# Bias of an attention kernel summed by VectorE from PSUM, maxima turned by VectorE, small products in reduced fp32

## The reference

```python
x = x + attention(_gn(x), W_qkv, W_out, b_out)
# attention, for one image, n = 4096 positions, c = 256 channels:
q, k, v = split(x @ W_qkv)                       # each n x c
k = softmax(k over the positions)
context = k.T @ v                                # c x c
out = (q @ context as in einsum('bde,bdn->ben')) @ W_out + b_out
```

## Time and profile before

| | |
|---|---|
| median of three runs | 1215.44 us |
| the profiled execution | 1214.93 us |
| its span, first to last instruction | 1213.2 us |
| PE busy | 1190.1 us, 98% of the span |
| DVE busy | 842.1 us, 69% |
| ACT busy | 840.1 us, 69% |
| POOL busy | 622.4 us, 51% |
| DMA | 63.5% of 16 engines' span, 220 GB/s |

### The profile page before, as it was taken

The page is one execution under the profiler, slowest core; times in us unless marked ns, Lnnn a source line. Parts: engine busy times, 40 slices in busy tenths (PEclk is TensorE's granted clock), DMA queues, the critical chain, the costliest instruction groups (busy, mean ns, idle before and its releaser), DMA issues.

```text
span 1213.2 us, 21447 instructions
## 1 busy us (share of the span) xinstructions
PE 1190.1 (98%) x8460; PEld 1115.8 (92%) x8460; DVE 842.1 (69%) x1582; ACT 840.1 (69%) x1140; POOL 622.4 (51%) x288
## 2 busy tenths in 40 slices
PE   4999999999999999999999999999999999999998
PEld 4998999999899998999989999899999989999897
DVE  6877667676776767768776677766767676676551
ACT  5767768677685776757677686776857768577664
POOL 8664564635645355563655636356463564536520
PEclk9999999999999999999999999999999999999999
DMA  9448666576765758666486665867657576573524
GB/s 339 146 167 294 218 235 205 195 269 208 274 203 199 264 172 294 226 206 237 162 301 229 221 227 183 286 209 252 204 201 263 193 278 225 201 252 122 191 74 170
DMA packets 107077, 266.71 MB, mean 220 GB/s; under 512 B 10208, under 2 KB 10208, under 8 KB 106976
## 3 DMA queue, kind: packets, MB, share of 16 engines
q1 hardware_dynamic: 106976, 265.33, 63.5%
HBM read 198.18 MB, written 67.11 MB: 219 GB/s over the span
## 4 chain that ended last, share of the span: by engine, by line
PE 93%; DVE 2%; ACT 1%; POOL 1%; DMA 1%; issue 1%; SPq 0%; DVEq 0%; POOLq 0%; ACTq 0%
PE ps_k L399 29%; PE ps_e L564 19%; PE ps_e L573 10%; PE ps_g L492 5%; PE ps_e L480 5%; PE ps_e L492 5%; PE ps_e L482 5%; PE ps_g L480 4%; PE ps_g L482 4%; PE ps_g L511 1%; PE ps_g L528 1%; PE ps_g L542 1%; PE ps_g L534 1%; POOL x_lo L347 1%; DVE mx L892 1%
## 5 line engine op out<-in xcount | busy, mean ns | idle before, releaser
L341 POOL TENSOR_TENSOR xt_lo<-xt_raw,xt_hi 128x1024 fp32r<-128x1024 f32 x128 | 307.4, 2404 | 434.5 <-ACT xt_hi L676 309.1
L347 POOL TENSOR_TENSOR x_lo<-x_raw,x_hi 128x1024 fp32r<-128x1024 f32 x128 | 281.4, 2216 | 65.6 <-ACT x_hi L681 56.2
L892 DVE TENSOR_TENSOR mx<-ps_k,mx 128x256 f32<-128x256 f32 x480 | 203.3, 424 | 95.8 <-ACT e_raw L685 74.3
L733 ACT ACTIVATE o_stage<-ps_e,bias 128x512 f32<-128x512 f32 x253 | 170.9, 689 | 114.1 <-PE ps_e L573 114.1
L399 PE MATMUL ps_k<-wk_hi,xt_hi 128*128 128x256 f32 x1024 | 207.1, 284 | 1.0 <-DVE mx L892 0.7
L399 PE MATMUL ps_k<-wk_lo,xt_hi 128*128 128x256 f32 x1024 | 205.5, 283 | 0.0
L685 ACT ACTIVATE e_raw<-ps_k 128x512 f32<-128x512 f32 x256 | 141.4, 596 | 87.2 <-PE ps_k L399 87.2
L849 DVE BATCH_NORM_STATS2 bn<-xs 128x6 f32<-128x512 f32 x240 | 154.5, 686 | 40.7 <-DMA xs<-in_xt_dram 39.5
L693 ACT ACTIVATE e_hi<-e_raw 128x1024 fp32r<-128x1024 f32 x128 | 135.1, 1055 | 60.9 <-DVE e_raw L917 33.0
L399 PEld LDWEIGHTS ps_k<-wk_hi,xt_hi 128*128 128x128 f32 x1024 | 163.4, 190 | 8.7 <-issue 1.8
L399 PE MATMUL ps_k<-wk_hi,xt_lo 128*128 128x256 f32 x1024 | 158.2, 283 | 0.0
(11 more groups left out here) (129 smaller groups left out, 1992.7 us busy)
## 6 DMA issues: line engine op xcount, KB each, us to landing
xt_raw<-in_xt_dram SPq DMA_DIRECT2D x128, 512.0 KB, 4.3
x_raw<-in_xn_dram SPq DMA_DIRECT2D x128, 512.0 KB, 3.5
out_dram<-o_stage SPq DMA_DIRECT2D x127, 512.0 KB, 4.5
xs<-in_xt_dram SPq DMA_DIRECT2D x240, 256.0 KB, 5.1
w_setup<-in_w_dram SPq DMA_DIRECT2D x2, 256.0 KB, 10.1
out_dram<-o_stage SPq DMA_DIRECT2D x2, 256.0 KB, 2.0
wk<-in_w_dram SPq DMA_DIRECT2D x1, 256.0 KB, 9.9
wq_t<-in_w_dram SPq DMA_DIRECT2D x1, 256.0 KB, 10.9
```

What stands on the lines that cost most here:

```text
L341: nc.gpsimd.tensor_tensor(xt_lo[:, s], xt_raw[:, s], xt_hi[:, s].bitcast(F32), ALU.subtract).then_inc(xt_lo_ready, 1)
L347: nc.gpsimd.tensor_tensor(x_lo[:, s], x_raw[:, s], x_hi[:, s, :, 0:C].bitcast(F32), ALU.subtract).then_inc(x_lo_ready, 1)
L733: nc.scalar.activation(o_stage[:, u % O_SLOTS, h, :], src, ACT.Identity, bias=bias[:, h:h + 1]).then_inc(o_ready, 1)
L892: nc.vector.tensor_tensor(mx[:], tile, mx[:], ALU.max).then_inc(max_done, 1)
```

## The change

- **Maxima.** DVE transposes `mx` itself, in squares of 32 x 32 (`nc.vector.transpose`), reduces each row of 32, brings the four quarters of the partitions together with three moves and reduces again. `m_blk` is now 32 partitions x 8. A move is a `tensor_reduce` over an axis of one element.
- **Spread.** DVE splits `m_blk` into two parts, one for fp32r and the rest, on 64 partitions, and multiplies them with two stacked identities (`block_diag`); PE spreads them with one fp32r product of 256 columns and ones.
- **Scales.** `dm` and `alpha` are made in the new layout, and four moves (`spread_scales`, before `take_first`) bring `alpha` back to channels on partitions.
- **Statistics.** For images from 1 on, mean and variance are split into two parts by DVE and averaged by one fp32r product each; `mean_of` and `var_of` add the two results.
- **Bias.** `bias_sum` is gone from PE. DVE scales the two rows of the matrix in PSUM with `neg_mean * rstd`, adds them, transposes, reduces, moves, adds b_out, and moves again.
- **Order.** On PE both `emit_high` of output 0 stand ahead of its `emit_low`. POOL waits for `diag_ready` of block 1 ahead of xt_low(n, 0), and of the next block 0 ahead of xt_low(n, 5). ACT makes four small copies at the start. In PE's stream `turn_max` is gone; the maxima wait for `turned_ready` on DVE's own side.
- `turned` and `b_terms` lie in the memory of `u_hi`, `diag` in its second half.

```diff
@@ gpsimd, period
+                pool.wait_ge(diag_ready, b * 2 + 2)
                 if more:
                     xt_low(n, np_, 0)
...
                     for j in range(3, NCH):
+                        if j == HALF + 1:
+                            pool.wait_ge(diag_ready, n * 2 + 1)
                         xt_low(n, np_, j)
@@ tensor
-            def turn_max(b, blk):
...
             def spread_max(b, blk):
...
+                pe.wait_ge(diag_ready, b * 2 + (blk + 1))
+                nc.tensor.matmul(max_psum(b, blk)[:, 1, 0:C], one_r[0:2 * Q].broadcast_to([2 * Q, P]), diag,
+                                 start=True, stop=True).then_inc(bc_ps, 1)
             def stats_mean(b):
...
+                    pe.wait_ge(max_done, b * (TILES * NCH))
+                    pe.wait_ge(mean_parts_ready, b)
+                    nc.tensor.matmul(stats_psum(b, 0), grp_r[:], mean_parts[:].rearrange("p k c -> p (k c)"), start=True,
+                                     stop=True).then_inc(mean_ps, 1)
             def stats_var(b):
...
+                    pe.wait_ge(var_parts_ready, b)
+                    nc.tensor.matmul(stats_psum(b, 1), grp_r[:], var_parts[:].rearrange("p k c -> p (k c)"), start=True,
+                                     stop=True).then_inc(var_ps, 1)
-            def bias_sum(b, parity):
...
                 emit_high(b, parity, 0, 0)
-                bias_sum(b, parity)
+                emit_high(b, parity, 0, 1)
                 emit_low(b, parity, 0, 0)
-                emit_high(b, parity, 0, 1)
                 emit_low(b, parity, 0, 1)
@@ vector
+            def move(to, values):
+
+                return nc.vector.tensor_reduce(to, values.unsqueeze(len(values.shape)), AX_X, ALU.max)
...
+                if b > 0:
+                    dve.wait_ge(mv_ready, b + 1)
+                    move(mean_parts[:, 0, :], mv[:, :, 0]).then_inc(mean_hi_ready, 1)
+                    dve.wait_ge(mean_hi_ready, b)
+                    nc.vector.tensor_tensor(mean_parts[:, 1, :], mv[:, :, 0], mean_parts[:, 0, :].bitcast(F32),
+                                            ALU.subtract).then_inc(mean_parts_ready, 1)
             def mean_of(b, parity):
...
+                    nc.vector.tensor_scalar(mean_rest[:], sums[:, CB:2 * CB], -1.0, None,
+                                            ALU.mult).then_inc(mean_rest_ready, 1)
+                    dve.wait_ge(mean_rest_ready, b)
+                    nc.vector.scalar_tensor_tensor(out=neg_mean[:, parity, :], in0=sums[:, 0:CB], scalar=-1.0,
+                                                   in1=mean_rest[:], op0=ALU.mult, op1=ALU.add).then_inc(mean_sum_ready, 1)
+                    dve.wait_ge(mean_sum_ready, b)
+                    nc.vector.tensor_tensor(dev[:], mv[:, :, 0], neg_mean[:, parity, :], ALU.add).then_inc(mean_read, 1)
...
+                if b > 0:
+                    dve.wait_ge(var2_ready, b + 1)
+                    move(var_parts[:, 0, :], var2[:]).then_inc(var_hi_ready, 1)
+                    dve.wait_ge(var_hi_ready, b)
+                    nc.vector.tensor_tensor(var_parts[:, 1, :], var2[:], var_parts[:, 0, :].bitcast(F32),
+                                            ALU.subtract).then_inc(var_parts_ready, 1)
             def block_max(b, blk):
...
+                n = b * 2 + blk + 1
+                dve.wait_ge(max_done, n * (TILES * HALF))
+                nc.vector.transpose(turned[:], mx[:]).then_inc(turned_ready, 1)
+                dve.wait_ge(turned_ready, n)
+                nc.vector.tensor_reduce(quad[:, :, 0], turned[:].rearrange("p (q k) -> p q k", k=Q), AX_X,
+                                        ALU.max).then_inc(quad_ready, 1)
+                dve.wait_ge(quad_ready, n)
+                for r in range(1, QUADS):
+                    last = move(quad[0:Q, :, r], quad[r * Q:(r + 1) * Q, :, 0])
+                last.then_inc(quad_moved, 1)
+                dve.wait_ge(quad_moved, n)
+                nc.vector.tensor_reduce(m_blk[:, blk, :], quad[0:Q], AX_X, ALU.max).then_inc(m_blk_ready, 1)
+
+            def block_diag(b, blk):
+                n = b * 2 + blk + 1
+                dve.wait_ge(m_blk_ready, n)
+                move(m_parts[0:Q, :], m_blk[:, blk, :]).then_inc(m_part_hi_ready, 1)
+                dve.wait_ge(m_part_hi_ready, n)
+                nc.vector.tensor_tensor(m_parts[Q:2 * Q, :], m_blk[:, blk, :], m_parts[0:Q, :].bitcast(F32),
+                                        ALU.subtract).then_inc(m_part_lo_ready, 1)
...
+                dve.wait_ge(m_part_lo_ready, n)
+                nc.vector.tensor_tensor(diag.rearrange("p (q k) -> p q k", k=Q),
+                                        eye2[:].unsqueeze(1).broadcast_to([2 * Q, NQ, Q]),
+                                        m_parts[:].bitcast(F32).unsqueeze(2).broadcast_to([2 * Q, NQ, Q]),
+                                        ALU.mult).then_inc(diag_ready, 1)
             def bias_of(b):
...
+                dve.wait_ge(scaled_mean_ready, b + 1)
+                nc.vector.tensor_scalar(b_terms[:, 0, :], ps_g0[:, 0, 0:C], scaled_mean[:, 0:1], None,
+                                        ALU.mult).then_inc(b_first_ready, 1)
+                dve.wait_ge(b_first_ready, b + 1)
+                nc.vector.scalar_tensor_tensor(out=b_terms[:, 0, :], in0=ps_g0[:, 1, 0:C], scalar=scaled_mean[:, 1:2],
+                                               in1=b_terms[:, 0, :], op0=ALU.mult, op1=ALU.add).then_inc(b_terms_ready, 1)
+                dve.wait_ge(b_terms_ready, b + 1)
+                nc.vector.transpose(b_terms[:, 1, :], b_terms[:, 0, :]).then_inc(b_turned_ready, 1)
...
             def gather_steps(b, parity, more):
                 n, np_ = b + 1, 1 - parity
                 block_max(b, 1)
+                block_diag(b, 1)
                 if more:
                     mean_of(n, np_)
                 block_scales(b)
-                mean_bias(b, parity)
                 shift(b, 4)
                 if more:
                     var_of(n)
                 e_low(b, 3)
                 shift(b, 5)
                 e_low(b, 4)
+                spread_scales(b)
                 take_first(b)
```

More of the change, by code:

```diff
@@ L107, in build @@
         u_lo = sb("u_lo", [P, CB, C], F32R)
+        with nc.sbuf_tensor("turned", [P, C], F32) as turned:
+            pass
+        with nc.sbuf_tensor("b_terms", [P, CB, C], F32) as b_terms:
+            pass
         u_hi = sb("u_hi", [P, CB, C], F32R)
+        diag = u_hi[0:2 * Q, 1, :]
         m_lo = u_lo
@@ L536, in combine_m @@
                     last.then_inc(m_ps, 1)
-            def bias_sum(b, parity):
-                pe.wait_ge(m_full_ready, b + 1)
-                for h in range(CB):
-                    for c in range(CB):
-                        last = nc.tensor.matmul(ps_g0[:, 0, h:h + 1], m_full[:, c, h * P:(h + 1) * P],
-                                                neg_mean[:, parity, c:c + 1], start=(h == 0 and c == 0),
-                                                stop=(c == CB - 1), skip_group_check=True)
-                last.then_inc(bias_ps, 1)
             def out_psum(b, u, h):
@@ L702, in scales @@
                 act.wait_ge(dm_ready, b + 1)
-                nc.scalar.activation(alpha[:], dm[:], ACT.Exp).then_inc(alpha_ready, 1)
+                nc.scalar.activation(alpha_q[:], dm[:], ACT.Exp).then_inc(alpha_q_ready, 1)
             def wk_high(b, parity):
@@ L739, in emit @@
                         emit_half(b, u, h)
+            act.wait_ge(consts_ready, 5)
+            nc.scalar.activation(grp_r[:], grp[:], ACT.Copy).then_inc(grp_r_ready, 1)
+            nc.scalar.activation(one_r[:], one_col[:], ACT.Copy).then_inc(one_r_ready, 1)
+            for r in range(2):
+                last = nc.scalar.activation(eye2[r * Q:(r + 1) * Q, :], ident[r * Q:(r + 1) * Q, r * Q:(r + 1) * Q],
+                                            ACT.Copy)
+            last.then_inc(eye2_ready, 1)
             for j in range(NCH):
@@ L908, in block_scales, with spread_scales @@
                 dve.wait_ge(m_all_ready, b + 1)
-                nc.vector.tensor_tensor(dm[:], m_blk[:], m_all[:].unsqueeze(1).broadcast_to([P, 2, CB]),
+                nc.vector.tensor_tensor(dm[:], m_blk[:], m_all[:].unsqueeze(1).broadcast_to([Q, 2, NQ]),
                                         ALU.subtract).then_inc(dm_ready, 1)
+            def spread_scales(b):
+                dve.wait_ge(alpha_q_ready, b + 1)
+                by_quad = alpha_q[:].rearrange("p k (d r) -> p k d r", r=QUADS)
+                for r in range(QUADS):
+                    last = move(alpha[r * Q:(r + 1) * Q, :, :], by_quad[:, :, :, r])
+                last.then_inc(alpha_ready, 1)
             def shift(b, j):
@@ L1105, in period @@
                 block_max(n, 0)
+                block_diag(n, 0)
                 bn_halves(8, 12)
```

157 lines of the change are left out of this document (105 added, 52 removed).

## The result

The changed kernel takes **1241.27 us** (median of 4 runs, 1237.64 to 1241.58), beside 1215.59 for the kernel before on the same chip: ratio 1.0209, 95% interval 1.0183 to 1.0234. One of the four executions of the kernel before took 4129.46 us and is left out of the ratio; the others lie between 1214.12 and 1215.74. The forecast was 1224, slower, with a range from 1199 to 1238: the sign was right, the size 17 us short, and the time lies outside the range. The profiled execution took 1241.58, its span is 1239.9.

A forecast was written before the change was run, and what follows sets the result against it. PE was taken to bound the kernel (93% of the chain). Per image +1.0 - 0.5 gave +7.7 over 14 images, image 15 +0.9, image 0 nothing: +8.6 on the median 1215.44, thus 1224 us, range 1199 to 1238.

The forecast's parts named there:

- Place one: Variance product: POOL's xt_low holds DVE's dev, so PE goes on 1.0 us later per image (bounds +0.7 to +1.5).
- Place two: Emission: bias chain of 3.4 us on DVE delays statistics and loads; PE still keeps 0.5 us an image.
- the landing of the loads: Third batch of xs loads, before the later outputs: lands 0.3 us later (bounds -0.6 to +1.3).
- the queue is full from there on: Emission: DMA is full behind the first output's store and the xt load, so the landing was taken as +0.3.
- My row for a full queue: Profile row cited for the loads: DMA at 0.99 of its time from 615 to 620 us.
- rival (c): Emission: bias chain delays the loads by its store, 1.3 us; +1.5 us per image, 1237 us, chance 0.18.
- PE's savings: Work PE no longer does: 2.1 us an image, 29 us over 14 images if nothing else ended later.
- the term for the spread: Spread of a maximum on PE: one pass of 0.12 to 0.15 us instead of 0.44, saving 0.3, twice an image.
- The mean product and the turn: PE in the gather: the turn's 0.2 us goes, and the mean product falls from 0.2 to 0.1.
- Start and end: Image 0: 0, with 2 us either way; image 15: +1.5 at the third output half, less 0.6 in its gather, +0.9.

The follow-up runs named there:

- e1: The changed kernel with POOL waiting for dm_ready instead of the second diagonal ahead of xt_low(n, 0): 1222.9 us.
- e10: The changed kernel with dev and the second of the variance's parts made by tensor_scalar instructions instead of tensor_tensor, POOL's wait unmoved: 1222.36 us.
- e3: The changed kernel with DVE's first four statistics moved ahead of take_second, from behind the bias and the second chunk's maxima: 1229.59 us.
- e5: e4 with the second four statistics loads (xs 4 to 7) issued by SP ahead of the emission loop, not behind the first output's store: 1201.87 us.
- e4: The changed kernel with the edits of e1 and e3 together: 1211.87 us, ratio 0.9973 to the kernel before.
- e7: e5 with the spread product on all 128 rows (added rows hold zeros) instead of 64: 1188.14 us, ratio 0.9774 to the kernel before.
- e12: The changed kernel with only the spread product put on all 128 rows instead of 64: 1237.6 us.
- e9: e7 with the second spread of image 0 on PE behind its third gather instead of inside the second: 1188.59 us.

## Why the prediction was right and wrong

**Place one: right.** The chain to the second diagonal took 2.46 us (658.26 to 660.72; I had 2.5), the transpose 0.44 (0.42), POOL started at 660.80 just behind it, and `dev` ended with POOL. From the end of e_low (642.03 before, 658.26 after) to PE's variance product it is 5.03 us before and 5.89 after: +0.86, with 1.0 forecast. e1 and e10 take this away by two different edits and bring 18.4 and 18.9 us. PE waited 1.09 where I wrote 1.6, mostly because it came later: the spread was hardly cheaper.

**Place two: the step that failed is the landing of the loads.** The bias chain took 3.4 us (616.05 to 619.46), as forecast, and in the middle images no PE wait came of it directly. But I took +0.3 for the third batch, since "the queue is full from there on". From DVE's first operation behind the M product, in the kernel before

```profile
598.75 0.88 DVE L982 SCALAR_TENSOR_TENSOR acc_hi<-ps_g,rstd,zero_eye 128x256 fp32r<-128x256 f32 x2 [0.49 <-PE ps_g L534]
```

to that batch's statistics (620.04) it is 21.29 us. In the changed kernel it is 23.51 (613.57 to 637.08): +2.2, outside my bounds of -0.6 to +1.3. The queue was not full. Here are stretches of 4 us from 6.3 us behind that operation on, with the DMA share second to last, before and then after:

```profile
605.00:609.00 4.00, 4.00 (x27) 3.58 (x26) 3.15 (x7) 1.71 (x3) 4.00 (x3) 1.00 0.92 313
609.00:613.00 4.00, 4.00 (x22) 3.31 (x21) 2.67 (x4) 2.71 (x5) 2.58 (x2) 1.00 0.98 282
```
```profile
620.00:624.00 4.00, 4.00 (x23) 3.36 (x22) 3.86 (x8) 2.78 (x6) 4.00 (x3) 1.00 0.71 253
624.00:628.00 4.00, 4.00 (x26) 3.54 (x25) 3.24 (x7) 2.60 (x4) 3.30 (x2) 1.00 0.67 194
```

My row for a full queue, was of 615 to 620 in the kernel before, over 16 us behind that operation. At the time when the second batch is issued there was room, and it was lost: that batch came late twice over, behind DVE's statistics (e3) and behind the store (e5). SP issued it 6.5 us behind the operation in the kernel before and 8.4 in the changed one:

```profile
605.25 3.27 SPq L249 DMA_DIRECT2D xs<-in_xt_dram  x4
```
```profile
622.00 2.18 SPq L298 DMA_DIRECT2D xs<-in_xt_dram  x4
```

The third batch was not issued later (14.3 us behind the operation, against 15.0), but it landed 9.2 us after its first issue instead of 6.3. The loads of xt behind them came late as well. I had named them, but no term of mine priced what that costs PE: ACT waited for one, and in this image PE's weight loads of the keys stood 0.56 us for xt_hi and 0.50 for xt_lo, ahead of the spread.

```profile
631.16 1.06 ACT L717 ACTIVATE xt_hi<-xt_raw 128x1024 fp32r<-128x1024 f32 x1 [1.17 <-DMA xt_raw<-in_xt_dram]
```

 My rival (c) had this mechanism, the loads delayed by the chain, at 1237 and with a chance of 0.18; it named the store and priced it at 1.3. In the image shown, PE's sixth output comes 29.89 us behind the operation instead of 28.49, +1.40. This is the dearest image: PE's wait for o_stage is 1.3 here, and at most 1.0 in the other middle images. Over the 14 the mean is what place one leaves of the 1.14, about +0.3, where I had -0.5. That is some 11 us of the miss; about 2 come back at place one.

**PE's savings: the term for the spread was mis-sized.** I priced the pass at half a key pair, 0.12 to 0.15; it cost 0.50 at the first place, more than the four passes (0.44) that it took the place of. In the gather, from the last high pass to the next gather behind the low part, before had 0.66 for the spread and the variance product, e4 0.62, and e7 0.23. The mean product and the turn saved the 0.3 that I took. So 1.46 an image instead of 2.1. This did little for the miss: by e12 the cheap spread is worth 3.7 us in the changed kernel, as PE waits right behind both. Beside e5 it is worth 13.7.

**Start and end: taken too lightly.** For image 0 I took 0 with 2 us either way, and what lies ahead of image 1's first spread was +7.3. PE's first product comes 1.1 later (16.4 against 15.3; over the kernels of this study it starts between 15.3 and 16.9). At the spread PE waits 3.5 where it waited 1.6 before. A wait of 1.9 for e_lo is new. In the changed kernel the granted clock falls behind these waits (columns: PE, PEld, DVE, ACT, POOL, clock, DMA share, GB/s):

```profile
57.00:65.00 8.00, 8.00 (x58) 8.00 (x58) 7.89 (x13) 4.74 (x6) 3.97 (x2) 0.83 0.41 131
65.00:75.00 10.00, 7.94 (x59) 7.53 (x58) 9.38 (x22) 6.79 (x8) 5.57 (x4) 0.92 0.64 215
```

In the kernel before it is 1.00 in both. In image 15 I took 0.6 off for the gather, and there PE waited 0.97 for its spread (1183.76). Behind it the bias came as late as forecast, but the third half of the output lost more than the 1.5 that I took:

```profile
1214.54 0.69 ACT L774 ACTIVATE o_stage<-ps_e,bias 128x512 f32<-128x512 f32 x1 [3.55 <-DVE bias L889]
...
1215.28 0.73 PE L608 MATMUL ps_e<-xt_hi,wk_hi 128*128 128x512 f32 x2 [2.23 <-ACT o_stage L774]
...
1217.63 1.05 PE L608 MATMUL ps_e<-xt_lo,wk_hi 128*128 128x512 f32 x2
1218.48 1.05 PE L617 MATMUL ps_e<-xt_hi,wk_lo 128*128 128x512 f32 x2
```

PE stands 2.2 us, and from 1216.78 to 1220.19 pairs take 0.85 instead of 0.47, as at the lower of the two levels (1.2 and 2.4 GHz); the granted clock of 1215 to 1220 is 0.68 on average. That is 3.4 us for 4 pairs that are 1.9 at the higher level, 1.5 more. No run takes the clock away by itself, so its share is read from these rows alone.

**The miss of 18.1 in parts:** start 7.3, middle 8.2 (place two some 11, less 2 at place one), end 2.6. The middle rests on runs (e1, e3, e5, e10, e12). The start and the end, 9.9 together, are read from rows; e9 moved the longest wait of the start and won nothing, so its cause stays open beyond DVE's queue.

## What to carry to other kernels

When work moves from the bounding engine to another one, follow what that engine releases, the loads most of all: a load queued in program order behind a store waits for whatever the store waits for. Let such loads go first, then move the work. The changed kernel became 53 us faster (1241.3 to 1188.1) by four small edits, two of the order on SP and DVE, one of a wait, one of a shape. A saving on the bounding engine counts only where nothing is late right behind it (the same edit was worth 3.7 us in the changed kernel and 13.7 where nothing was late). And take the first and last iteration apart, engine by engine: here they carried 10.8 of 26.7 us.

## What was not expected of the hardware

- A product of 64 rows between products of 128 rows cost 0.50 us of PE's time, one of 128 rows with zeros in it 0.12; the row of its own duration (0.38 against 0.28) shows only a part.
- A DVE operation with two tensors from SBUF is held while POOL's xt_low runs: 2073 ns for `dev`, against two of 210 with the second operand as the partition's scalar.
- In the changed kernel PE's waits of 3.5, 1.9 and 2.2 us were followed by stretches of lower granted clock (0.83, 0.91 and 0.68 on average); the one behind the 2.2 cost 1.5 us. Behind those of 1.1 to 1.3 us in the middle images it was 1.00.
- A DVE transpose of 128x256 in fp32 takes 440 ns, as much as a copy of that size (421).
